# Attention of a fused kernel: sixteen ScalarE exponentials with the row minimum as bias in place of four GpSimd subtractions and four wide exponentials

## The chip, the cores and the metric

The kernel runs on one core of a Trainium2 chip. The metric is the device time of one execution in microseconds, as the median of several runs. The times quoted from the profile come from one profiled execution.

## The reference

The whole computation is a chain of four residual layers on an image `x` of 128 x 128 positions and 64 channels: `x = x + layer(group_norm(x))`. The change lies in the first, an attention along each row of the image with 4 heads of 32:

```python
x = _layernorm(pair, gamma, beta)
q = (x @ Wq).reshape(B, L, L, N_HEAD, D_HID) * SCALING
k = (x @ Wk).reshape(B, L, L, N_HEAD, D_HID)
v = (x @ Wv).reshape(B, L, L, N_HEAD, D_HID)
bias = x @ Wb
gate = jax.nn.sigmoid(x @ Wg + bg)
attn = jnp.einsum('bijhd,bikhd->bijkh', q, k)
attn = attn + bias[:, None]
attn = jax.nn.softmax(attn, axis=-2)
out = jnp.einsum('bijkh,bikhd->bijhd', attn, v).reshape(B, L, L, N_HEAD * D_HID)
out = gate * out
return out @ Wo + bo
```

For each of 128 image rows and each head there is a 128 x 128 matrix of scores, and a softmax over its last axis. All of it is fp32.

## The kernel before

The function `layer0_attention` works on groups of `ROWS` = 4 image rows; there are `GROUPS` = 32 of them. Each engine has its own program, and the programs are held together by semaphores alone. The order of instructions on each engine is written out by hand. In its iteration g an engine works on up to three groups: scores and exponentials of group g, the weighing and the sums of group g - 1, and gate and output of group g - 2.

Of one group:

- TensorE makes the scores of 4 rows and 4 heads (L823, `scores`) into `quad`, one bank for each head.
- VectorE takes head by head (L733, `shift_head`). Four instructions of 128x128 compute bias minus score, write it to `prob` and write the minimum of each line to a column of `least`. After four rows the semaphore `shifted` counts up. This is the negated score, so its minimum is the score's maximum, and the exponential takes `scale=-1.0`.
- GpSimd subtracts the minimum from a whole head, four rows in one instruction of 128x512 (L669), in place in `prob`, and counts `lowered`.
- ScalarE takes the exponential of a whole head, 128x512, in place (L697, `exponentials`), and counts `exps_done`.
- TensorE transposes the probabilities row by row (L831, `turn`), four heads to a bank, with two banks for four rows. ScalarE copies each bank to `pT` (L692, `keep_turn`). The turn of rows 2 and 3 waits for the copies of rows 0 and 1. For row 0, `turn` waits for `exps_done` of head after head.
- TensorE weighs the values (L837, `weigh`) and adds up the probabilities (L845, `add_up`). The sums are transposed (L865), VectorE takes their reciprocals (L756), GpSimd widens them to 128x512 in `rwide` (L675), and TensorE transposes them once more (L876).
- VectorE makes the gate's factor and the gated result (L766, L772), TensorE the output projection (L890), VectorE the residual sum (L778), its statistics (L796) and sums by cell (L797). GpSimd copies the two halves of the finished rows to a second image with the halves swapped (L684).
- For the next group TensorE makes q and k (L807, `project_qk`), which ScalarE keeps with a bias column (L701, L703, `keep_qk`). Gate and v (L813, L816, `project_gv`) go into the same two banks as the turns. ScalarE takes tanh of the gate's half (two of 128x256 with a bias column, L722), and VectorE adds the bias to v (L785) after that tanh.

ScalarE's order in an iteration is: four `keep_turn` of group g - 1, the exponentials of head 0 of group g, `keep_qk(g + 1)`, the exponentials of head 1, the two tanh, the exponentials of heads 2 and 3. TensorE's order is: scores of g, transpose of the sums of g - 2, turns of g - 1, transposes of `rwide`, q and k of g + 1, gate and v of g, output projection of g - 2, weighing and sums of g - 1. GpSimd's order before the change is: subtraction of head 0, the widening for g - 2, subtractions of heads 1 to 3, the two swaps of g - 2.

Of the kernel before, what the change touches and what calls it, by code (L numbers as in the profile page):

```python
# [9 lines left out]
ALU = mybir.AluOpType  # L10
ACT = mybir.ActivationFunctionType
# [3 lines left out]
L = 128  # L15
C = 64
HEADS, HD = 4, 32
ROWS = 4
GROUPS = L // ROWS
# [583 lines left out]
def layer0_attention(nc, m):  # L603
# [11 lines left out]
    prob = [m.nat[:, b * WIDE:(b + 1) * WIDE] for b in range(2)]  # L615
# [5 lines left out]
    least = [m.take(HEADS * ROWS) for _ in range(2)]  # L621
    sums = m.take(128)
    rtotal = m.take(ROWS * HEADS)
    rwide = m.take(CH)
    S = lambda name: m.sem(f"l0_{name}")
    bias_kept, bias_made = S("bias_kept"), S("bias_made")
    qk_made, q_ready, k_ready = S("qk_made"), S("q_ready"), S("k_ready")
    gv_made, v_ready, th_ready = S("gv_made"), S("v_ready"), S("th_ready")
    scores_made, shifted, lowered, exps_done = S("scores_made"), S("shifted"), S("lowered"), S("exps_done")
    turned, kept = S("turned"), S("kept")  # L630
    av_made, sums_made, sums_kept, sums_turned = S("av_made"), S("sums_made"), S("sums_kept"), S("sums_turned")
    rtotal_ready, rwide_ready, r_made, factor_ready, gated_ready = S("rtotal_ready"), S("rwide_ready"), S("r_made"), S("factor_ready"), S("gated_ready")
# [5 lines left out]
    def at(r, h, w=L):  # L638
        return slice((r * HEADS + h) * w, (r * HEADS + h + 1) * w)
# [4 lines left out]
    def of_head(t, h):  # L644

        return t.rearrange("p (r h x) -> p h r x", r=ROWS, h=HEADS)[:, h, :, :]
# [8 lines left out]
    def by_half(t):  # L655
        return t.rearrange("p (h x) -> p h x", h=2)

    with nc.Block() as block:

        @block.gpsimd  # L660
        def _(pool):
            step = m.chain(pool, "pool")
            for g in range(STEPS0):
                b = g % 2
                for h in range(HEADS):
                    if g < GROUPS:
                        pool.wait_ge(shifted, HEADS * g + h + 1)
                        scored = of_head(prob[b], h)
                        pool.tensor_tensor(scored, scored, of_head(least[b], h).broadcast_to([128, ROWS, L]),  # L669
                                           ALU.subtract).then_inc(lowered, 1)  # L670
                    if h == 0 and g >= 2:
                        pool.wait_ge(rtotal_ready, g - 1)
                        if g > 2:
                            pool.wait_ge(r_made, g - 2)
                        pool.tensor_copy(rwide.rearrange("p (x d) -> p x d", d=HD),  # L675
                                         rtotal.unsqueeze(2).broadcast_to([128, ROWS * HEADS, HD])).then_inc(rwide_ready, 1)
                if g >= 2:
                    pool.wait_ge(rwide_ready, g - 1)
                    if g < GROUPS:
                        pool.wait_ge(lowered, HEADS * (g + 1))  # L680
                    pool.wait_ge(x1_ready, g - 1)
                    for e in range(2):
                        there, here = slice(e * C, (e + 1) * C), slice((1 - e) * C, (2 - e) * C)
                        step(pool.tensor_copy(m.pairs(HALF * (g - 2), HALF, m.x1s)[there], m.pairs(HALF * (g - 2), HALF)[here]))  # L684

        @block.scalar
        def _(act):
            def keep_turn(g, r):
                act.wait_ge(turned, 4 * g + r + 1)
                if r == 0 and g > 0:  # L690
                    act.wait_ge(sums_made, g)
                act.activation(pT[r], m.bank[r % 2][:, :], ACT.Copy).then_inc(kept, 1)  # L692

            def exponentials(g, b, h):
                act.wait_ge(lowered, HEADS * g + h + 1)
                t = of_head(prob[b], h)
                act.activation(t, t, ACT.Exp, scale=-1.0).then_inc(exps_done, 1)  # L697

            def keep_qk(g):
                act.wait_ge(qk_made, g + 1)  # L700
                act.activation(by_half(qT[g % 2]), m.quad[:, 0:2, 0:256], ACT.Identity,  # L701
                               bias=m.qkg_bias[:, 0:1]).then_inc(q_ready, 1)
                act.activation(by_half(kT[g % 2]), m.quad[:, 0:2, 256:512], ACT.Identity,  # L703
                               bias=m.qkg_bias[:, 1:2]).then_inc(k_ready, 1)

            keep_qk(0)
            for g in range(GROUPS + 1):
                own, past = g < GROUPS, g >= 1
                if past:
                    for r in range(ROWS):  # L710
                        keep_turn(g - 1, r)
                if own:
                    exponentials(g, g % 2, 0)
                if g + 1 < GROUPS:
                    keep_qk(g + 1)
                if own:
                    exponentials(g, g % 2, 1)
                    act.wait_ge(gv_made, g + 1)
                    if g >= 2:
                        act.wait_ge(factor_ready, g - 1)  # L720
                    for half, bank in enumerate((turn_a, turn_b)):
                        last = act.activation(th[g % 2][:, half * 256:(half + 1) * 256], bank[:, 0:256], ACT.Tanh, scale=0.5,  # L722
                                              bias=m.qkg_bias[:, 2:3])
                    last.then_inc(th_ready, 1)
                    exponentials(g, g % 2, 2)
                    exponentials(g, g % 2, 3)
# [1070 lines left out]
def build(nc, args, out):  # L1797
    with ExitStack() as ctx:
        m = Memory(nc, ctx)
        load_and_prepare(nc, m, args)  # L1800
        group_norm(nc, m, 0)
        layer0_norm(nc, m)
        layer0_attention(nc, m)
        layer1(nc, m)
        layer2(nc, m, args)
        layer3(nc, m, args, out)
# [23 lines left out]
```

## Time and profile before

| | |
|---|---|
| median of 3 runs | 1188.38 us (1185.97 to 1188.86) |
| the profiled execution | 1187.14 us |
| its span, first to last instruction | 1185.3 us |
| mean granted TensorE clock | 0.945 |
| busy: TensorE, VectorE, ScalarE, GpSimd | 1092.6, 743.1, 520.7, 341.0 us |
| attention stage | about 104 to 404 us |

The busy shares are averages over four layers with different limits; a change to one layer is read from the stretch of that layer. In the profile PE is TensorE's matmuls, PEld its weight loads (which overlap them), DVE is VectorE, ACT is ScalarE and POOL is GpSimd. Ends of matmuls are modelled, and neighbouring instructions of one engine can overlap, so that two instructions in a row may take less than twice the time of one. What stands in brackets at the end of a row is the idle time of the engine before it, and who ended it.

### The profile page before, as it was taken

The page shows a single profiled execution, that of the slowest core. Times are in us where ns is not written, and L with a number is a line of the kernel's source. Part 1 is how long each engine was busy: PE and PEld are TensorE (multiplying, and loading weights), DVE is VectorE, ACT ScalarE, POOL GpSimd, SP SyncE. Part 2 cuts the span into 40 slices and gives each one's busy share as a digit, 9 for nine tenths or more (in the row PEclk, how much of TensorE's full clock was granted, in tenths as well). Part 3 has the DMA queues.
Part 4 walks back from the last instruction along what each step waited for, and adds up shares of the span by engine and source line. Part 5 has one row for each costly group of instructions (what it writes and reads, how often), then busy time and mean ns, then how long its engine had stood idle before and what let it go on. Part 6 is the DMA issues. An engine that isn't in the chain of part 4 may idle for free. (4 is left out here: it accounts for less than half of the span.)

```text
span 1185.3 us, 25594 instructions
## 1 busy us (share of the span) xinstructions
PE 1092.6 (92%) x9547; PEld 783.1 (66%) x9547; DVE 743.1 (63%) x3576; ACT 520.7 (44%) x1113; POOL 341.0 (29%) x477
## 2 busy tenths in 40 slices
PE   4898999999999699949999999999999999999688
PEld 3457777777777334437767777677677677677486
DVE  3673777778778522245676676766766766766235
ACT  2364767676676300024444445444444444443200
POOL 0151656665665210000221221221212212212211
PEclk8796999999999889958999999999999999999869
DMA  8000000000000000000000000000000000000012
GB/s 165 1 1 1 2 3 2 2 3 2 2 3 2 1 1 1 1 10 1 1 1 1 2 1 2 1 1 1 1 1 2 1 1 1 1 1 1 1 40 108
DMA packets 10463, 11.09 MB, mean 9 GB/s; under 512 B 3812, under 2 KB 8164, under 8 KB 10340
## 3 DMA queue, kind: packets, MB, share of 16 engines
q1 hardware_dynamic: 8964, 8.87, 2.8%
q8 instruction: 76, 1.25, 0.4%
q10 hardware_dynamic: 1376, 0.59, 0.3%
q14 instruction: 47, 0.39, 0.1%
HBM read 5.14 MB, written 4.23 MB: 8 GB/s over the span
## 5 line engine op out<-in xcount | busy, mean ns | idle before, releaser
L1498 PE MATMUL quad<-theta,nat 128*128 128x512 f32 x512 | 240.7, 593 | 0.0
L669 POOL TENSOR_TENSOR nat<-nat,arena 128x512 f32<-128x512 f32 x128 | 132.6, 1047 | 127.2 <-DVE arena L733 127.2
L1297 POOL TENSOR_TENSOR nat<-nat,const 128x512 f32<-128x512 f32 x32 | 40.6, 1270 | 439.8 <-DVE nat L1436 439.8
L1506 PEld LDWEIGHTS quad<-flat 128*128 128x128 f32 x768 | 104.6, 190 | 46.4 <-ACT flat L1328 25.0
L1498 PEld LDWEIGHTS quad<-theta,nat 128*128 128x128 f32 x512 | 87.5, 191 | 61.7 <-issue 61.7
L1506 PE MATMUL quad<-flat 128*128 128x128 f32 x768 | 123.8, 284 | 2.8 <-ACT flat L1328 1.7
L733 DVE CUSTOM_DVE_ANT_0 nat<-quad,arena 128x128 f32<-128x128 f32 x512 | 113.2, 282 | 7.0 <-PE quad L823 7.0
L1328 ACT ACTIVATE flat<-quad 128x256 f32<-128x256 f32 x192 | 73.3, 382 | 70.6 <-PE quad L1506 56.7
L692 ACT ACTIVATE nat<-bank 128x512 f32<-128x512 f32 x128 | 69.5, 595 | 56.9 <-PE bank L831 56.9
L1405 DVE SCALAR_TENSOR_TENSOR flat<-nat,c,duo 128x128 f32<-128x128 f32 x64 | 22.1, 345 | 101.9 <-PE duo L1515 101.9
L697 ACT ACTIVATE nat<-nat 128x512 f32<-128x512 f32 x128 | 77.3, 634 | 5.6 <-POOL nat L669 5.5
L831 PE MATMUL bank<-const,nat 128*128 128x128 f32 x512 | 69.9, 279 | 8.8 <-ACT nat L692 8.0
L1494 PE MATMUL bank<-nat 128*128 128x128 f32 x512 | 69.2, 279 | 0.3 <-DVE nat L1482 0.3
L831 PEld LDWEIGHTS bank<-const,nat 128*128 128x128 f32 x512 | 55.8, 141 | 18.8 <-ACT nat L692 15.6
L1494 PEld LDWEIGHTS bank<-nat 128*128 128x128 f32 x512 | 63.5, 195 | 0.9 <-DVE nat L1482 0.7
L1386 ACT ACTIVATE nat<-bank 128x512 f32<-128x512 f32 x32 | 19.1, 597 | 87.2 <-PE bank L1603 87.2
L1421 DVE MAX8 arena<-nat 128x8 f32<-128x128 f32 x128 | 27.9, 281 | 44.5 <-ACT nat L1365 44.5
L1453 DVE CUSTOM_DVE_ANT_0 nat<-nat,duo 128x128 f32<-128x128 f32 x128 | 29.2, 283 | 37.4 <-PE duo L1614 37.4
L733 DVE DVE_READ_ACCUMULATOR2_ANT arena<- 128x1 f32 x512 | 42.3, 83 | 0.0
L1310 POOL COPY img<-flat 64x256 f32<-64x256 f32 x64 | 39.6, 619 | 3.9
L807 PE MATMUL quad<-flat,w 64*128 64x256 f32 x256 | 38.2, 419 | 2.3 <-DVE arena L733 2.0
L1410 DVE SCALAR_TENSOR_TENSOR flat<-flat 128x128 f32<-128x128 f32 x64 | 38.3, 599 | 2.2
(390 smaller groups left out, 2271.8 us busy)
## 6 DMA issues: line engine op xcount, KB each, us to landing
out<-nat SPq DMA_DIRECT2D x16, 256.0 KB, 2.0
const<-in_constants ACTq DMA_DIRECT2D x1, 400.5 KB, 3.2
arena<-in_L_conv_Ws SPq DMA_DIRECT2D x1, 240.0 KB
flat<-arena SPq DMA_DIRECT2D x3, 32.0 KB, 4.5
nat<-in_x SPq DMA_DIRECT2D x4, 0.2 KB, 12.0
arena<-in_L_conv_Wq ACTq DMA_DIRECT2D x1, 32.0 KB, 6.7
arena<-in_L_conv_Wk ACTq DMA_DIRECT2D x1, 32.0 KB, 6.4
arena<-in_L_conv_Wv ACTq DMA_DIRECT2D x1, 32.0 KB, 6.1
```

What stands on the lines that cost most here:

```text
L669: pool.tensor_tensor(scored, scored, of_head(least[b], h).broadcast_to([128, ROWS, L]), ALU.subtract).then_inc(lowered, 1)
L692: act.activation(pT[r], m.bank[r % 2][:, :], ACT.Copy).then_inc(kept, 1)
L697: act.activation(t, t, ACT.Exp, scale=-1.0).then_inc(exps_done, 1)
L733: last = dve.tensor_tensor_reduce(prob[b][:, at(r, h)], m.quad[:, h, row(r)], m.bias[:, row(h)], -1.0, BIG, ALU.add, ALU.min, least[b][:, ...
L831: last = pe.transpose(m.bank[r % 2][:, row(h)], prob[g % 2][:, at(r, h)], ident)
L1297: pool.tensor_tensor(quarters(rem), quarters(rem), ident.unsqueeze(1).broadcast_to([128, ROWS, 128]), ALU.add).then_inc(diag_added, 1)
L1310: step(pool.tensor_copy(m.cols3[:, :, ROWS * r + e:ROWS * (r + 1):2].rearrange("p j t -> p t j"), source))
L1328: act.activation(kept, m.quad[:, HALF * half:HALF * (half + 1), place * C:(place + 2) * C], ACT.Copy).then_inc(z_ready[half], 1)
L1410: dve.scalar_tensor_tensor(out=x_of(g, half), in0=held[half], scalar=0.0, in1=x_of(g, half), op0=ALU.max, op1=ALU.add).then_inc(x3_ready[h ...
L1494: last = pe.matmul(B[0][:, col(n)], source[:, col(n)], source[:, col(n)], start=True, stop=True)
L1498: return pe.matmul(m.quad[:, n, :], vT[:, col(n)], m.theta[:, part, :], start=(part == 0), stop=False, skip_group_check=True)
L1506: last = pe.matmul(m.quad[:, row, place * C:(place + 2) * C], a8[g % 2][:, col(row)], zs[half][k % 2][:, n, :], start=False, stop=(k == 2) ...
```

## The change

GpSimd's four subtractions of a group are left out, and with them the semaphore `lowered`. ScalarE now waits for VectorE's `shifted` and takes, for each head, four exponentials of 128x128, one for each row, each with that row's column of `least` as the bias: exp(-t + minimum). `exps_done` counts up after the fourth. GpSimd's widening of the reciprocals and its two swap copies stay, in the same order.

```diff
-                for h in range(HEADS):
-                    if g < GROUPS:
-                        pool.wait_ge(shifted, HEADS * g + h + 1)
-                        scored = of_head(prob[b], h)
-                        pool.tensor_tensor(scored, scored, of_head(least[b], h).broadcast_to([128, ROWS, L]),
-                                           ALU.subtract).then_inc(lowered, 1)
-                    if h == 0 and g >= 2:
-                        pool.wait_ge(rtotal_ready, g - 1)
-                        if g > 2:
-                            pool.wait_ge(r_made, g - 2)
-                        pool.tensor_copy(rwide.rearrange("p (x d) -> p x d", d=HD),
-                                         rtotal.unsqueeze(2).broadcast_to([128, ROWS * HEADS, HD])).then_inc(rwide_ready, 1)
                 if g >= 2:
+                    pool.wait_ge(rtotal_ready, g - 1)
+                    if g > 2:
+                        pool.wait_ge(r_made, g - 2)
+                    pool.tensor_copy(rwide.rearrange("p (x d) -> p x d", d=HD),
+                                     rtotal.unsqueeze(2).broadcast_to([128, ROWS * HEADS, HD])).then_inc(rwide_ready, 1)
                     pool.wait_ge(rwide_ready, g - 1)
-                    if g < GROUPS:
-                        pool.wait_ge(lowered, HEADS * (g + 1))
                     pool.wait_ge(x1_ready, g - 1)
...
             def exponentials(g, b, h):
-                act.wait_ge(lowered, HEADS * g + h + 1)
-                t = of_head(prob[b], h)
-                act.activation(t, t, ACT.Exp, scale=-1.0).then_inc(exps_done, 1)
+                act.wait_ge(shifted, HEADS * g + h + 1)
+                for r in range(ROWS):
+                    t = prob[b][:, at(r, h)]
+                    last = act.activation(t, t, ACT.Exp, scale=-1.0, bias=least[b][:, at(r, h, 1)])
+                last.then_inc(exps_done, 1)
```

## Rows read from the trace of the kernel before

**Rows 1.** Stretch: PE, PEld, DVE, ACT, POOL busy, granted clock, DMA share, GB/s.

```profile
229.86:238.82 8.96, 8.44 (x145) 6.77 (x141) 7.12 (x42) 6.23 (x13) 5.45 (x8) 1.00 0.01 2
```

**Rows 2.** Waits of TensorE, 120 to 388 us: total, times, longest.

```profile
PE duo L876 <- POOL arena L675: 8.1, 30, 0.3
PE bank L831 <- ACT nat L692: 7.5, 30, 0.3
```

**Rows 3.** Groups of instructions, 120 to 388 us: busy, mean ns, idle before.

```profile
L697 ACT ACTIVATE nat<-nat 128x512 f32<-128x512 f32 x121 | 73.0, 634 | 0.1
L692 ACT ACTIVATE nat<-bank 128x512 f32<-128x512 f32 x120 | 65.1, 595 | 54.7 <-PE bank L831 54.7
...
L669 POOL TENSOR_TENSOR nat<-nat,arena 128x512 f32<-128x512 f32 x120 | 124.5, 1047 | 100.2 <-DVE arena L733 100.2
```

**Rows 4.** ScalarE in order of time, one repeat: start us, us, instruction.

```profile
231.76 1.09 ACT L692 ACTIVATE nat<-bank 128x512 f32<-128x512 f32 x2 [1.58 <-PE bank L831]
233.11 1.09 ACT L692 ACTIVATE nat<-bank 128x512 f32<-128x512 f32 x2 [0.26 <-PE bank L831]
234.09 0.62 ACT L697 ACTIVATE nat<-nat 128x512 f32<-128x512 f32 x1
235.60 0.69 ACT L701 ACTIVATE arena<-quad,qkg_bias 128x512 f32<-128x512 f32 x1 [0.89 <-PE quad L807]
...
236.75 0.63 ACT L697 ACTIVATE nat<-nat 128x512 f32<-128x512 f32 x1
237.27 0.84 ACT L722 ACTIVATE arena<-bank,qkg_bias 128x256 f32<-128x256 f32 x2
237.98 1.17 ACT L697 ACTIVATE nat<-nat 128x512 f32<-128x512 f32 x2
```

**Rows 5.** TensorE in order of time, the same repeat.

```profile
231.13 1.04 PE L831 MATMUL bank<-const,nat 128*128 128x128 f32 x8
232.41 1.15 PE L831 MATMUL bank<-const,nat 128*128 128x128 f32 x8 [0.25 <-ACT nat L692]
233.83 0.66 PE L876 MATMUL duo<-const,arena 128*128 128x128 f32 x4 [0.27 <-POOL arena L675]
234.42 1.13 PE L807 MATMUL quad<-flat,w 64*128 64x256 f32 x8
...
238.82 1.17 PE L823 MATMUL quad<-arena 32*128 32x128 f32 x32
```

**Rows 6.** GpSimd in order of time, the same repeat.

```profile
232.18 1.05 POOL L669 TENSOR_TENSOR nat<-nat,arena 128x512 f32<-128x512 f32 x1 [2.26 <-DVE arena L733]
233.17 0.61 POOL L675 COPY arena<-arena 128x512 f32<-128x512 f32 x1
```

**Rows 7.** ScalarE's shorter copies in other stages: one group, two in order of time.

```profile
L1328 ACT ACTIVATE flat<-quad 128x256 f32<-128x256 f32 x192 | 73.3, 382 | 70.6 <-PE quad L1506 56.7 <-PE quad L1498 12.5
...
413.32 0.51 ACT L1106 ACTIVATE nat<-arena 64x128 f32<-64x128 f32 x2
413.54 0.29 ACT L1106 ACTIVATE nat<-arena 64x128 f32<-64x128 f32 x1
```

**Rows 8.** VectorE in order of time, from v to the end of an iteration.

```profile
238.14 0.76 DVE L785 TENSOR_TENSOR arena<-bank,v_bias 128x256 f32<-128x256 f32 x2 [0.60 <-ACT arena L722]
...
239.50 0.40 DVE L797 TENSOR_REDUCE flat<-img 128x4 f32<-128x256 f32 x1
```

**Rows 9.** ScalarE at both ends of the stage: groups 0, 1, 30, 31.

```profile
113.87 0.63 ACT L697 ACTIVATE nat<-nat 128x512 f32<-128x512 f32 x1
...
116.76 1.09 ACT L692 ACTIVATE nat<-bank 128x512 f32<-128x512 f32 x2 [0.50 <-PE bank L831]
...
124.22 1.09 ACT L692 ACTIVATE nat<-bank 128x512 f32<-128x512 f32 x2 [1.00 <-PE bank L831]
...
384.20 1.09 ACT L692 ACTIVATE nat<-bank 128x512 f32<-128x512 f32 x2 [1.58 <-PE bank L831]
...
392.18 1.08 ACT L692 ACTIVATE nat<-bank 128x512 f32<-128x512 f32 x2 [1.18 <-PE bank L831]
```

More of the change, by code:

```diff
@@ L628, in layer0_attention @@
     gv_made, v_ready, th_ready = S("gv_made"), S("v_ready"), S("th_ready")
-    scores_made, shifted, lowered, exps_done = S("scores_made"), S("shifted"), S("lowered"), S("exps_done")
+    scores_made, shifted, exps_done = S("scores_made"), S("shifted"), S("exps_done")
     turned, kept = S("turned"), S("kept")
```

## The prediction

> **What bounds the kernel now.** I read the stretches of the attention stage first, then the groups and the waits inside it, then one group of four rows in order of time. In the steady part the stage repeats itself every 8.96 us. TensorE is busy for 8.44 us of each repeat at a granted clock of 1.00, VectorE for 7.12, ScalarE for 6.23, GpSimd for 5.45 [rows 1]. TensorE's missing 0.52 us are two waits, 30 times each: 0.25 us for ScalarE's copies of the turned probabilities (L692), and 0.27 us for GpSimd's widening of the reciprocals (L675) [rows 2]. So TensorE sets the repeat. ScalarE idles 2.73 us of it, 1.84 of them ahead of L692 and 0.89 ahead of L701 [rows 3, 4].
>
> I measure a repeat from the start of the first L692, called zero (231.76) [rows 4]. ScalarE then runs four copies, with one short wait, until the first exponential at 2.33. It waits for the next group's q and k until 3.84, keeps them until 4.99, takes the second exponential (0.52), the two tanh (0.71) and the last two exponentials, and is through at 7.39 (1.17 after 6.22). The next zero is at 8.965: slack is 1.58. TensorE's transposes begin 0.63 before zero [rows 4, 5].
>
> **What is removed.** GpSimd loses 4 subtractions a group, 1047 ns each [rows 3], 4.2 us a group and 134 us over 32 groups. None of them is the last wait of ScalarE in the steady part: L697's idle there is 0.1 us over 121 instructions [rows 3]. What they do hold is L675. The widening starts at 233.17, right behind the subtraction that began at 232.18, and TensorE's transposes of it start at 233.83 instead of at the end of the turns before them (232.41 + 1.15 = 233.56) [rows 5, 6]. Without the subtraction the widening is ready about 1 us sooner, so this 0.27 us wait goes. With ScalarE out of the way the repeat would be 8.965 - 0.27 = 8.69 us. As TensorE starts a matmul some 0.07 us before the modelled end of the one before it, its later work moves up by up to 0.34.
>
> **What is added.** ScalarE does 16 exponentials of 128x128 a group instead of 4 of 128x512; the elements are the same, the fixed cost is paid 12 times more and each instruction reads its bias from a column of SBUF. No row before has this form. What counts is the distance between the starts of two neighbours, called e here.
> - Elements: copies from PSUM take 595 ns at 512 columns and 382 at 256 [rows 3, 7], 0.832 ns a column, 0.107 us for 128.
> - From the exponentials of now: neighbours start 0.52 to 0.53 us apart (1.17 - 0.634 for the pair, and 0.52 from 236.75 to 237.27). Taking off 384 columns, 0.32, leaves 0.205. The bias: two L701/L703 copies with a bias column take 1.15, 0.575 each, against 0.49 for L692 without one (1.09 - 0.60), so 0.085 more. Together e = 0.29 [rows 3, 4].
> - From the tanh, which have a bias column: 0.71 for two of 256 columns, 0.355 each, less 0.107 is 0.248; they read PSUM, and SBUF against PSUM is 0.035 more (0.525 against 0.49): 0.283 [rows 4].
> - Bounds: 0.248, the tanh without the SBUF term, from below. From above 0.22, the distance of two short copies from SBUF without a bias on 64 partitions [rows 7], plus 0.09 for the bias: 0.31.
> I take 0.29, to which two of the three ways lead. One such instruction alone lasts about 0.634 - 0.32 + 0.09 = 0.40, so the last of a head ends 0.11 after the next could have started.
>
> ScalarE's work grows by 16 x 0.29 - 4 x 0.525 = 2.54 us a group. It had 2.73 us idle, but the idle time doesn't lie where the work goes: the engine takes its instructions in order, and its loop closes over TensorE. Turn of row 0 needs the last exponential of head 3; the first L692 needs that turn; everything else on ScalarE is queued behind it.
>
> **The new repeat, along ScalarE.** From zero: first head of exponentials at 2.33. They no longer wait for GpSimd, and VectorE has had head 0 done long before. They end their slots at 2.33 + 4e = 3.49. q and k of the next group come from TensorE 0.34 sooner, at 3.84 - 0.34 = 3.50, so they no longer hold ScalarE noticeably. Then 1.15 for L701 and L703, 4e, 0.71 for the tanh, 8e, 0.11 for the tail. From the end of an exponential to the first L692: TensorE starts within 0.06 of a ScalarE end (the first L692, of 0.60, ends at 232.36, and the turn that waits for its bank starts at 232.41). The fourth transpose of row 0 starts about 0.33 behind the first (an estimate: eight take 1.04 with the length of the last), at 231.46, and L692 follows at 231.76, 0.30 later [rows 3 to 5]: together 0.36. The sum is 3.50 + 1.15 + 0.71 + 0.11 + 0.36 + 12e = 5.83 + 12e = 9.31. Where q and k are there already it is 2.33 + 1.15 + 0.71 + 0.47 + 16e = 4.66 + 16e = 9.30. Either way ScalarE's loop is longer than TensorE's 8.69, and by it the new repeat is 0.345 us longer than 8.965.
>
> What waits behind: VectorE's L785 needs the tanh, which now end at 3.50 + 1.15 + 1.16 + 0.83 = 6.64. From L785's start to L797's end are 1.76 [rows 8], so VectorE turns to the next scores at 8.4; they are done 8.23 - 0.34 = 7.89 after zero (238.82 + 1.17 in before's times) [rows 5]. Its first two heads then are through some 2 us later, at 1.2 of the next repeat, while ScalarE wants the second at 4.65. VectorE has over 2 us free in 9.31, so it isn't on the path. GpSimd keeps the widening and the two swaps, no bound. TensorE waits once a repeat, for the last exponentials, some 0.6 us, with the work of scores and sums behind it and nothing else delayed.
>
> **The ends of the stage** [rows 9]. First group: the second head of exponentials starts at 113.87 whatever happens before it, as it is behind q and k. Then 12e + 0.71 + 0.47 = 4.66, so the first L692 is at 118.53 instead of 116.76: +1.77. The next interval was 7.46 with no older group's work in it and becomes 4.66 + 16e = 9.30: +1.84. The 29 intervals from 124.22 to 384.20 average 8.965 and become 9.31: +10.0. The last has no q and k to keep: 2.33 + 0.71 + 0.47 + 16e = 8.15 against 392.18 - 384.20 = 7.98: +0.17. Behind it nothing changes. The sum is +13.8 us. The profiled execution took 1187.14 us (span 1185.3), so it would take 1200.9. The median of the runs is 1188.38, 1.24 more; the forecast is 1188.38 + 13.8 = 1202 us.
>
> The time hangs on e with 12 + 16 + 29 x 12 + 16 = 392 of them: 0.01 us is 3.9 us. At e = 0.255 the change is worth nothing.
>
> The Trainium skill, "ScalarE: Activation LUTs", section "What ACT_TABLE_LOAD costs", gives an instruction with a bias column 280 ns and 0.833 ns a column, with neighbours overlapping by about 93 ns. By that estimate e would be 0.294 and the sum +15.4 instead of +13.8. The trace before agrees at 256 columns (0.477 alone would be 0.493 by the page), and has no 128x128 exponential.
>
> **The rivals.**
> 1. Forecast, e from 0.27 to 0.30: 1194 to 1206 us, chance 0.70. Three derivations fall in it.
> 2. Short instructions have a longer floor, as the copies of 128 columns at 0.22 without any bias hint [rows 7]. At e = 0.31 the second form governs, 4.66 + 16 x 0.31 = 9.62: +7.8 for the 392 and +2.0 for 29 intervals at 0.07 more, 1212 us. Against it: those copies have a strided output and 64 partitions. Chance 0.13.
> 3. The bias costs what it costs in the tanh, and SBUF nothing: e = 0.248 to 0.264, 1185.6 to 1192. The removed GpSimd wait and the longer queue cancel. Chance 0.10, most of it within 0.3%.
> 4. The other side: the fetch of the bias is hidden wholly behind the neighbour, e about 0.22 as in those copies. Below 0.255 the change wins, and below 0.239 TensorE's 8.69 bounds again: 29 x -0.275 = -8.0, the start +0.9 and +0.7, 1182 us. For it speaks that a freed wait of 0.27 stands plainly in the trace; against it that L701 and L692, of equal shape, differ by 0.085 between starts, not only in length. Chance 0.07.
> A fall of TensorE's clock through the longer wait gets no chance of its own: its busy share would go from 8.44 of 8.96 us, at a clock of 1.00 [rows 1], to 8.44 of 9.31.
>
> **Chances and range.** Three in a thousand, 3.6 us, is about what a measurement of this kernel can tell from no change. Rivals 1 and 2 are slower by more, 0.83; rival 3 gives 0.08 to the same and 0.01 to either side; rival 4 is faster. So faster 0.08, same 0.08, slower 0.84. The range runs from e = 0.264 (1192) to just below the upper bound's 1212: 1191 to 1211. It leaves out rival 4, most of 3, and the tip of 2.
>
> **What would show it.** Right: first L692 of neighbouring groups 9.2 to 9.4 us apart; exponentials of 128x128 0.28 to 0.30 between starts and about 0.40 long; ScalarE nearly without idle time (some 0.5 us a repeat) and all of it ahead of the first L692; a new wait of TensorE's L831 for ScalarE's exponentials, 0.5 to 0.7 us a group; its wait for L675 gone; VectorE's L733 unchanged. Wrong: neighbours closer than 0.255, then TensorE's wait for the exponentials is small or absent; or VectorE later than I have it, its heads then ending the waits of the exponentials.

## The result and the profile after

The changed kernel takes 1205.08 us (median of 4 runs, 1203.96 to 1206.08), the kernel before 1188.11 us (4 runs). The ratio is 1.0146, with a 95% interval from 1.0128 to 1.0163: 17 us slower. The forecast was 1202, the range 1191 to 1211. The profiled execution after took 1205.16 us, its span is 1203.4.

One repeat of the attention stage after the change, as a stretch (busy PE, PEld, DVE, ACT, POOL, then the granted clock), beside [rows 1]:

```profile
270.03:279.41 9.38, 8.45 (x143) 6.77 (x142) 6.95 (x44) 8.71 (x25) 1.41 (x3) 1.00 0.01 3
```

The repeat went from 8.965 to 9.38 us. TensorE does the same work in it, 8.45 us against 8.44. ScalarE went from 6.23 to 8.71 us, and GpSimd from 5.45 to 1.41. Four microseconds a repeat were taken from an engine whose busy time bounded nothing; only the place of the widening in its order held TensorE up.

The groups of instructions and the waits of TensorE in the steady part, 120 to 398 us, beside [rows 2, 3] (L689 is the new exponential, L683 the copy that was L692, L824 the turn that was L831):

```profile
L689 ACT ACTIVATE nat<-nat,arena 128x128 f32<-128x128 f32 x472 | 147.1, 397 | 0.0
L683 ACT ACTIVATE nat<-bank 128x512 f32<-128x512 f32 x119 | 64.8, 596 | 20.4 <-PE bank L824 20.4
...
PE bank L824 <- ACT nat L689: 20.0, 29, 0.7
...
PE bank L824 <- ACT nat L683: 7.3, 29, 0.3
```

Each exponential lasts 397 ns. ScalarE's only idle time is ahead of L683, and TensorE has a new wait for L689, 0.69 us in each of 29 groups. The wait for the widened reciprocals is gone from the list.

ScalarE in order of time, from one zero to the next, beside [rows 4]:

```profile
270.03 1.09 ACT L683 ACTIVATE nat<-bank 128x512 f32<-128x512 f32 x2 [0.42 <-PE bank L824]
271.37 1.09 ACT L683 ACTIVATE nat<-bank 128x512 f32<-128x512 f32 x2 [0.26 <-PE bank L824]
272.36 1.26 ACT L689 ACTIVATE nat<-nat,arena 128x128 f32<-128x128 f32 x4
273.52 0.67 ACT L694 ACTIVATE arena<-quad,qkg_bias 128x512 f32<-128x512 f32 x1
274.10 0.68 ACT L696 ACTIVATE arena<-quad,qkg_bias 128x512 f32<-128x512 f32 x1
274.67 1.27 ACT L689 ACTIVATE nat<-nat,arena 128x128 f32<-128x128 f32 x4
275.83 0.82 ACT L715 ACTIVATE arena<-bank,qkg_bias 128x256 f32<-128x256 f32 x2
276.55 2.44 ACT L689 ACTIVATE nat<-nat,arena 128x128 f32<-128x128 f32 x8
279.41 1.09 ACT L683 ACTIVATE nat<-bank 128x512 f32<-128x512 f32 x2 [0.42 <-PE bank L824]
```

This is the loop of the prediction. Head 0 starts at 2.33 and takes 1.16, q and k follow without a wait, and the last exponential ends at 8.96. The next zero comes 0.42 later. Neighbouring exponentials start (2.44 - 0.397) / 7 = 0.292 us apart.

TensorE at the end of that loop, beside [rows 5]:

```profile
277.87 0.49 PE L824 MATMUL bank<-const,nat 128*128 128x128 f32 x3
279.04 0.77 PE L824 MATMUL bank<-const,nat 128*128 128x128 f32 x5 [0.69 <-ACT nat L689]
280.06 1.15 PE L824 MATMUL bank<-const,nat 128*128 128x128 f32 x8 [0.25 <-ACT nat L683]
281.04 0.60 PE L869 MATMUL duo<-const,arena 128*128 128x128 f32 x4
```

Three transposes of row 0 run as soon as the sums are turned, and the fourth, that of head 3, waits 0.69 us. This row shows what bounds: of the exponentials, TensorE waits only for the last of sixteen.

### The profile page after: what moved, and what is told of

Read it like the earlier page. It is cut to its first block and busy times, and to the rows that moved or that the text cites. A ratio compares the mean times of both kernels' runs of the same rounds, so it can differ in the third digit from the quotient of the medians.

```text
span 1203.4 us, 25821 instructions
## 1 busy us (share of the span) xinstructions
PE 1096.7 (91%) x9547; PEld 785.2 (65%) x9547; DVE 737.9 (61%) x3576; ACT 600.0 (50%) x1497; POOL 211.8 (18%) x349
## 5 line engine op out<-in xcount | busy, mean ns | idle before, releaser
L689 ACT ACTIVATE nat<-nat,arena 128x128 f32<-128x128 f32 x512 | 159.4, 397 | 3.4 <-DVE arena L726 3.4
L824 PE MATMUL bank<-const,nat 128*128 128x128 f32 x512 | 78.3, 287 | 30.9 <-ACT nat L689 22.0
L824 PEld LDWEIGHTS bank<-const,nat 128*128 128x128 f32 x512 | 55.9, 142 | 48.7 <-ACT nat L689 29.7
L683 ACT ACTIVATE nat<-bank 128x512 f32<-128x512 f32 x128 | 69.8, 596 | 22.4 <-PE bank L824 22.4
L778 DVE TENSOR_TENSOR arena<-bank,v_bias 128x256 f32<-128x256 f32 x64 | 24.2, 419 | 50.3 <-ACT arena L715 50.3
L675 POOL COPY img<-img 64x256 f32<-64x256 f32 x64 | 25.5, 398 | 155.3 <-DVE img L771 153.3
L669 POOL COPY arena<-arena 128x512 f32<-128x512 f32 x32 | 19.5, 610 | 134.8 <-issue 93.8
L1387 ACT ACTIVATE arena<-arena 128x4 f32<-128x4 f32 x32 | 6.6, 205 | 68.2 <-DVE arena L1450 68.2
## 6 DMA issues: line engine op xcount, KB each, us to landing
nat<-in_x SPq DMA_DIRECT2D x4, 0.2 KB, 12.1
```

The lines of the kernel that those rows point to most:

```text
L689: last = act.activation(t, t, ACT.Exp, scale=-1.0, bias=least[b][:, at(r, h, 1)])
L824: last = pe.transpose(m.bank[r % 2][:, row(h)], prob[g % 2][:, at(r, h)], ident)
```

## The experiments

Each run is compared with the kernel before on the same chip. The median of before was 1188.09 us beside the removal, the splitting, the order on GpSimd and the first version with k on VectorE, and 1187.1 us beside two and three split heads, the second version with k on VectorE and the wide first group. "Zero" is, as in the prediction, the start of a group's first copy of turned probabilities on ScalarE.

### The removal alone

This kernel leaves out the subtraction of the minimum altogether.

```diff
 # on the changed kernel
-                for r in range(ROWS):
-                    t = prob[b][:, at(r, h)]
-                    last = act.activation(t, t, ACT.Exp, scale=-1.0, bias=least[b][:, at(r, h, 1)])
-                last.then_inc(exps_done, 1)
+                t = of_head(prob[b], h)
+                act.activation(t, t, ACT.Exp, scale=-1.0).then_inc(exps_done, 1)
```

> The changed kernel with four wide exponentials of 128x512 a group again, without a bias: the subtraction of the minimum is left out of the computation altogether. This is the removal alone. My theory (TensorE bounds once ScalarE is out of the way, and only the wait for the widening went): a repeat of 8.69 us instead of 8.965, some 30 times, 1188 - 8 = 1180 us, TensorE without a wait for L675's successor, VectorE's instructions as long as before. Rival (GpSimd's subtractions slow VectorE or others through shared memory access): VectorE's L733 successor shorter than 281 ns, and more than 10 us gained. Second rival (the widening's wait hides another one right behind it): 1188, no gain.

Measured: 1172.29 us, ratio 0.9861 (0.9842 to 0.988). That is 16 us less, twice what was expected, so the expected size was wrong. The first rival asks for shorter VectorE instructions, and there are none: L724, the renamed L733, takes 282 ns on average in the steady part, as L733 does before. The gain is in the distance between TensorE's starts, which the run "Only the order on GpSimd" shows below.

### The splitting alone

```diff
 # on the kernel before
-                t = of_head(prob[b], h)
-                act.activation(t, t, ACT.Exp, scale=-1.0).then_inc(exps_done, 1)
+                for r in range(ROWS):
+                    t = prob[b][:, at(r, h)]
+                    last = act.activation(t, t, ACT.Exp, scale=-1.0)
+                last.then_inc(exps_done, 1)
```

> The kernel before, with GpSimd's subtractions, but each wide exponential split into four of 128x128 without a bias column. This is the splitting alone. My theory: neighbours start about 0.205 us apart (0.292 measured with the bias, less 0.085); ScalarE's loop is 2.33 + 1.15 + 0.72 + 0.11 + 0.42 + 16 x 0.205 = 8.0 us, under 8.965, so the time stays within 0.3% of 1188. Rival (the number of instructions is the cost, bias or not): starts 0.27 or more apart, the loop 9.1 or more, 1192 us or more.

Measured: 1187.73 us, ratio 0.9996 (0.9985 to 1.0007), no change. Two rows of ScalarE in order of time:

```profile
237.61 0.90 ACT L698 ACTIVATE nat<-nat 128x128 f32<-128x128 f32 x4
...
239.12 1.71 ACT L698 ACTIVATE nat<-nat 128x128 f32<-128x128 f32 x8
```

Four more exponentials take 1.71 - 0.90 = 0.81 us, 0.2025 each. So the splitting costs ScalarE 16 x 0.2025 - 4 x 0.525 = 1.14 us a group. Its idle time takes this in: ahead of the first copy it fell from 1.58 to 0.75 us, ahead of the copy of q from 0.89 to 0.62, and the time didn't move. The bias column accounts for 0.292 - 0.2025 = 0.09 us of an exponential, 1.43 us a group. Laid end to end without any wait for q and k, ScalarE's loop over TensorE is 2.33 + 1.15 + 0.71 + 0.11 + 0.42 + 4 x 0.525 = 6.82 us with wide exponentials. With the splitting it is 7.96, still under the repeat of 8.965; with the bias as well it is 9.39, over it. No run has the bias without the splitting.

### Only the order on GpSimd

```diff
 # on the kernel before, in GpSimd's program
+                if g >= 2:
+                    pool.wait_ge(rtotal_ready, g - 1)
+                    ... the widening, as in the changed kernel
                 for h in range(HEADS):
                     if g < GROUPS:
                         ... the subtraction
-                    if h == 0 and g >= 2:
-                        ... the widening
```

> The kernel before with one move on GpSimd: the widening of the reciprocals stands ahead of the subtraction of head 0 instead of behind it. Four wide exponentials and four subtractions as before. My theory: the 0.27 us wait of TensorE goes, the subtraction of head 0 starts about 0.6 us later and is still through before ScalarE is free for it at 2.33 after zero; a repeat of 8.69, 1180 us. Rival (the later subtractions now hold ScalarE's heads 0 to 2, or the gain of the change's removal needs GpSimd to be empty): a new idle time ahead of ScalarE's exponentials and 1185 us or more.

Measured: 1173.19 us, ratio 0.9874 (0.9854 to 0.9894). That is 15 us less with all four subtractions in place, as much within the noise as the 16 us without any. Here too the expected size, 8 us, was half of what came. Its zeros, and TensorE between them:

```profile
233.82 1.09 ACT L692 ACTIVATE nat<-bank 128x512 f32<-128x512 f32 x2 [1.58 <-PE bank L831]
...
242.30 1.09 ACT L692 ACTIVATE nat<-bank 128x512 f32<-128x512 f32 x2 [1.58 <-PE bank L831]
```

```profile
234.48 1.14 PE L831 MATMUL bank<-const,nat 128*128 128x128 f32 x8 [0.25 <-ACT nat L692]
235.46 0.60 PE L876 MATMUL duo<-const,arena 128*128 128x128 f32 x4
235.99 1.13 PE L807 MATMUL quad<-flat,w 64*128 64x256 f32 x8
```

The repeat is 8.48 us, not 8.69. From the second turn to the transposes of the widened reciprocals there are now 0.98 us between starts against 233.83 - 232.41 = 1.42 before, and from there to q and k 0.53 against 0.59 [rows 5]: 0.50 us in all for a wait that the list of waits gave 0.27. The idle column counts from the modelled end of the turn. Now the transposes start 0.16 us ahead of that end (234.48 + 1.14 = 235.62). Before, they started 0.27 behind it, and they took 0.66 us instead of 0.60. So here the matmul that waits also loses the overlap with its predecessor. With 0.49 instead of 0.27 a repeat, 30 times, the sum is 14.7 us, what the two runs show.

### How many heads can be split

On the kernel with only the order on GpSimd changed, the first n heads are done as in the changed kernel and the others as before. GpSimd subtracts for the heads from n on only; that part is not shown.

```diff
+                t = of_head(prob[b], h)
+                if h < n:
+                    act.wait_ge(shifted, HEADS * g + h + 1)
+                    for r in range(ROWS):
+                        t = prob[b][:, at(r, h)]
+                        last = act.activation(t, t, ACT.Exp, scale=-1.0, bias=least[b][:, at(r, h, 1)])
+                    last.then_inc(exps_done, 1)
+                else:
+                    act.wait_ge(lowered, (HEADS - n) * g + h - n + 1)
+                    act.activation(t, t, ACT.Exp, scale=-1.0).then_inc(exps_done, 1)
```

> Between the two kernels, with the widening first on GpSimd: heads 0 and 1 take four exponentials with the minimum as bias each, heads 2 and 3 keep GpSimd's subtraction and the wide exponential. My theory (ScalarE's loop is 6.82 us for no such head, and 0.64 us more for each, against 8.475 us of TensorE as measured in widening_first): 8.10 us, still hidden, so 1173 us as widening_first. Rival (the cost of the splitting is in proportion to the number of split heads, wherever the bound lies): half of the way from 1173 to 1205, 1189 us.

> As two_heads_bias with head 2 split too, head 3 alone with the subtraction. My theory: ScalarE's loop is 6.82 + 3 x 0.64 = 8.74 us and sets the repeat, 0.27 above TensorE's 8.475: about 1181 us, TensorE's first wait for an exponential back with some 0.3 us. Rival in proportion: 1197 us. Second rival (still hidden): 1173 us.

Measured: two heads 1174.99 us, ratio 0.9894 (0.9876 to 0.9912); three heads 1183.37 us, ratio 0.996 (0.9945 to 0.9974). Zeros of the kernel with two split heads, then of that with three:

```profile
228.28 1.09 ACT L692 ACTIVATE nat<-bank 128x512 f32<-128x512 f32 x2 [0.82 <-PE bank L838]
...
236.75 1.08 ACT L692 ACTIVATE nat<-bank 128x512 f32<-128x512 f32 x2 [0.81 <-PE bank L838]
```

```profile
231.72 1.08 ACT L692 ACTIVATE nat<-bank 128x512 f32<-128x512 f32 x2 [0.42 <-PE bank L838]
...
240.46 1.08 ACT L692 ACTIVATE nat<-bank 128x512 f32<-128x512 f32 x2 [0.42 <-PE bank L838]
```

The repeats are 8.47 and 8.74 us: TensorE's own with two, and 6.82 + 3 x 0.64 = 8.74 of ScalarE's loop with three. With two the first copy still finds ScalarE idle for 0.8 us, so the loop has slack. With three the idle time is down to 0.42, which is the turn-round over TensorE, the same as with four. The wait of TensorE that was expected there shows at its weight loads (8.3 us in 30 groups), not ahead of a matmul. The heads are not in proportion: the first two cost some 2 us of the total, if anything, the third 8, the fourth 22. Most of the last is 0.64 us in each of 29 intervals, and the start of the stage, below, has a share in it.

### Taking load off ScalarE in the changed kernel

```diff
 # on the changed kernel, ScalarE: its copy of k is left for group 0 alone
+                if g == 0:
+                    ... the copy of k
 # VectorE, ahead of head 3
+                if g + 1 < GROUPS:
+                    dve.wait_ge(q_ready, g + 2)
+                    dve.tensor_scalar(by_half(kT[(g + 1) % 2]), m.quad[:, 0:2, 256:512], m.qkg_bias[:, 1:2], None,
+                                      ALU.add).then_inc(k_ready, 1)
```

> The changed kernel with its sixteen exponentials, but the copy of k with its bias (0.57 us between starts) moved from ScalarE to VectorE, ahead of VectorE's head 3, for all groups but the first. My theory (ScalarE's loop of 9.38 us sets the repeat): 9.38 - 0.57 = 8.81 us, 31 times, so 1205 - 17 = 1188 us, with TensorE's wait for the exponentials down from 0.69 us to about 0.1. Rival (VectorE, later than before, is what really delays the exponentials): it gets 0.7 us more work, so no gain or a loss, 1205 us or more, and ScalarE idle ahead of its exponentials.

Measured: 1196.35 us, ratio 1.0064 (1.0047 to 1.0081). Half of the expected gain is missing: the expectation of 1188 us was wrong. VectorE in order of time, and then TensorE:

```profile
234.54 0.75 DVE L769 TENSOR_SCALAR arena<-quad,qkg_bias 128x512 f32<-128x512 f32 x1 [0.52 <-ACT arena L694]
...
236.05 0.48 DVE L776 SCALAR_TENSOR_TENSOR img<-duo,bo,img 128x256 f32<-128x256 f32 x1
```

```profile
236.59 1.08 PE L843 MATMUL duo<-nat,pick 128*32 128x128 f32 x32 [0.48 <-DVE img L776]
```

Here VectorE first waits 0.52 us for ScalarE to have read q, then copies k, then does head 3 and only then the residual sum, which TensorE's sums of the next group wait for, 0.48 us in 27 groups. The repeat is 9.165. The second version puts the residual sum ahead of the copy of k and leaves all else alone:

> k_on_vector with VectorE's order mended: the residual sum first, then the copy of k, then head 3. In k_on_vector the residual sum came late, and TensorE waited 0.48 us a repeat for it (repeat 9.165). My theory (ScalarE's loop bounds once that wait is gone): 9.38 - 0.57 = 8.81 us, 31 times, about 1188 us. Rival (VectorE simply has too much work for a shorter repeat): another of its results is waited for and the repeat stays above 9.0, 1194 us or more.

Measured: 1187.83 us, ratio 0.9998 (0.9988 to 1.0008). Its zeros, and a wait of TensorE between 125 and 380 us:

```profile
232.46 1.08 ACT L683 ACTIVATE nat<-bank 128x512 f32<-128x512 f32 x2 [0.45 <-PE bank L829]
...
241.29 1.08 ACT L683 ACTIVATE nat<-bank 128x512 f32<-128x512 f32 x2 [0.46 <-PE bank L829]
...
PE quad L821 <- DVE arena L727: 8.2, 28, 0.3
```

8.83 us here, for 8.81 expected. ScalarE's loop set the repeat of the changed kernel: taking 0.57 us out of it brought 17 us of time. That the repeat stopped so near 8.81 is in part chance, though. TensorE's wait for the exponentials is gone from the steady part, and instead its scores (L821) wait 0.29 us in each of 28 groups for VectorE's head 3, now behind the copy of k. So a loop over VectorE of 8.83 us bounds here, just over ScalarE's 8.81, and by these rows a larger cut on ScalarE alone would have brought little more.

### The start of the stage

In the profile after, the zeros of groups 0 and 1 lie 10.20 us apart, where the steady repeat is 9.38. In the stretches around them the seventh column is the granted clock:

```profile
116.00:118.00 2.00, 0.70 (x3) 0.34 (x3) 1.75 (x13) 2.00 (x8) 0.00 (x0) 1.00 0.00 0
118.00:120.00 2.00, 1.40 (x6) 1.17 (x7) 2.00 (x21) 1.18 (x4) 0.00 (x0) 0.59 0.00 0
120.00:122.00 2.00, 2.00 (x10) 1.53 (x11) 0.38 (x4) 1.39 (x3) 0.00 (x0) 0.56 0.00 0
```

TensorE is busy for 0.70 of 2 us, and behind that its clock is for the most part at the lower level (0.50 of full speed, 1.2 GHz) for some 4 us; from 122 us on it is 1.00 again. The experiment does group 0 alone in the old way (subtractions on GpSimd, wide exponentials); nothing else differs from the changed kernel.

> The changed kernel, but group 0 alone is done as before: four subtractions on GpSimd and four wide exponentials. In the changed kernel the first interval between the zeros of groups 0 and 1 is 10.20 us against 9.38 later, with TensorE's granted clock at 0.56 to 0.59 from 118 to 122 us. My theory (the long wait of TensorE in the first group takes the clock down, and that costs the 0.8 us): the first zero comes 1.8 us sooner, TensorE's wait of 0.84 us there goes, the clock stays at 1.00 and the next interval is 9.4; together 2.6 us less than the changed kernel, 1202.5 us. Rival (the fall of the clock has nothing to do with that wait): the interval stays at 10.2 and the gain is 1.8 us.

Measured: 1201.13 us, ratio 1.011 (1.0093 to 1.0128), 4 us under the changed kernel. The zeros of groups 0 and 1:

```profile
118.07 1.09 ACT L688 ACTIVATE nat<-bank 128x512 f32<-128x512 f32 x2 [0.50 <-PE bank L834]
...
127.45 1.09 ACT L688 ACTIVATE nat<-bank 128x512 f32<-128x512 f32 x2 [0.42 <-PE bank L834]
```

9.38 us apart, and the clock is at 1.00 in each stretch from 116 us on. That fits the theory; the 4 us of the medians, between forecasts of 2.6 and 1.8, don't decide by themselves. But the first version with k on VectorE had the fall as well (waits of 0.82 and 0.84 us in TensorE's first group), while the second, with waits of 0.95 and 0.84 us, had a clock of 1.00 from 114 us on. Two further kernels waited longer at one time and didn't fall either: two split heads 1.27 us, three split heads 1.45 us. The stretch of the first of them is nearly as idle as that of the changed kernel:

```profile
116.00:118.00 2.00, 0.73 (x10) 0.62 (x7) 1.43 (x9) 1.57 (x4) 0.00 (x0) 1.00 0.00 0
118.00:120.00 2.00, 1.75 (x15) 1.27 (x15) 2.00 (x21) 1.67 (x4) 0.07 (x1) 1.00 0.00 0
```

So the changed kernel itself was run twice more.

> The changed kernel itself once more, for the start of the stage alone. If TensorE's wait in the first group always takes the clock down behind it, the interval between the zeros of groups 0 and 1 is again 10.2 us, with a clock of some 0.5 to 0.6 for about 3 us. Rival (the wait only makes the fall possible, as k_on_vector and k_on_vector_late hint, of which one fell and the other did not): 9.4 us and a clock of 1.00 in at least one of two more executions.

> As changed_again_1, a further execution with a profile: 10.2 us by the theory that the wait always takes the clock down, 9.4 us possible by its rival.

Measured: 1204.2 and 1204.14 us. First two zeros of the one and of the other, with a stretch of each in which the clock is down:

```profile
117.56 1.09 ACT L683 ACTIVATE nat<-bank 128x512 f32<-128x512 f32 x2 [0.42 <-PE bank L824]
...
127.81 1.08 ACT L683 ACTIVATE nat<-bank 128x512 f32<-128x512 f32 x2 [0.42 <-PE bank L824]
...
118.00:120.00 2.00, 1.79 (x8) 1.57 (x8) 0.97 (x10) 1.24 (x3) 0.00 (x0) 0.50 0.00 0
```

```profile
119.57 1.09 ACT L683 ACTIVATE nat<-bank 128x512 f32<-128x512 f32 x2 [0.42 <-PE bank L824]
...
129.92 1.09 ACT L683 ACTIVATE nat<-bank 128x512 f32<-128x512 f32 x2 [0.42 <-PE bank L824]
...
122.00:124.00 2.00, 2.00 (x10) 1.64 (x12) 0.00 (x0) 1.76 (x5) 0.00 (x0) 0.52 0.00 0
```

10.25 and 10.35 us: in all three executions the clock fell behind the first group and the interval was about 0.9 us over the steady one. TensorE's first wait was 1.12, 0.62 and 0.39 us in them, its second 0.84 each time. So for the changed kernel the fall and its price are shown, and in the one execution with a wide first group it didn't come. That the waits as such cause it is not shown: the first two waits come to 1.23 to 1.96 us in the executions that fell and to 1.52 to 1.79 in the three kernels that did not, and the busy share of the stretch doesn't tell them apart either. What does stays open.

## Why the prediction was right

The direction, the place and the mechanism were right; the sum was 13.8 us where the stage grew by 17.1 (from the first copy of q in the stage, 105.07 before and 105.43 after, to the last zero, 392.18 and 409.62). The rows of after for the terms (those of before are in [rows 9]), then term by term:

```profile
105.43 0.69 ACT L694 ACTIVATE arena<-quad,qkg_bias 128x512 f32<-128x512 f32 x1 [10.53 <-PE quad L800]
...
119.11 0.60 ACT L683 ACTIVATE nat<-bank 128x512 f32<-128x512 f32 x1 [0.56 <-PE bank L824]
...
129.31 1.09 ACT L683 ACTIVATE nat<-bank 128x512 f32<-128x512 f32 x2 [0.42 <-PE bank L824]
...
401.39 1.09 ACT L683 ACTIVATE nat<-bank 128x512 f32<-128x512 f32 x2 [0.42 <-PE bank L824]
...
409.62 1.09 ACT L683 ACTIVATE nat<-bank 128x512 f32<-128x512 f32 x2 [0.42 <-PE bank L824]
```

| term | predicted | measured |
|---|---|---|
| first zero later | +1.77 | (119.11 - 105.43) - (116.76 - 105.07) = +1.99 |
| zeros of groups 0 and 1 | +1.84 | 10.20 - 7.46 = +2.74 |
| 29 intervals | +10.0 | 272.08 - 259.98 = +12.1 |
| last interval | +0.17 | 8.23 - 7.98 = +0.25 |

- **The distance e** was taken as 0.29 and is 0.292. It came out of rows of other forms: the element rate from two copies, the fixed part from the wide exponentials (0.205 without the bias, measured 0.2025), and 0.085 for the bias from L701 against L692, measured 0.09. The Trainium skill, "ScalarE: Activation LUTs", section "What ACT_TABLE_LOAD costs", gives 280 ns with a bias column and 186 ns without one, 0.833 ns a column with either, and 93 ns of overlap between neighbours. An estimate by these figures is 0.294 us with the bias and 0.200 without. The runs agree, with 0.292 and 0.2025. The bound of 0.31 from the short strided copies was too high, that of 0.248 too low.
- **The loop over TensorE** of 4.66 + 16e is the step that made the difference between "ScalarE has 2.73 us idle and gets 2.54 more" and a loss. It was confirmed in both directions, by two and three split heads and by the copy of k taken away. Of its terms one was mis-sized: from the end of the last exponential to the zero I had 0.36, and it is 0.42. The 0.30 in it was read where the transposes flow without a wait; behind a wait they take 0.37 (279.04 to 279.41). With some rounding that is 0.07 us a repeat, 2.1 us in 29, two thirds of the 3.3 us that the sum was short by.
- **The slack of 1.58** in the prediction is misread. Of the 1.58 us ahead of zero 0.42 are the turn-round, which no work can fill, and the 0.89 ahead of the copy of q can be filled in part. The slack of the loop is 8.965 - 6.82 = 2.15 us, and the change took 2.57. This cost the forecast nothing, as its sum goes by the loop.
- **The start** was right in its first part: 1.77 predicted, 1.99 measured, of which 0.14 are the clock, already down at 118.60 (in the two repeats the first zero is 13.54 and 13.53 us behind the first copy of q, here 13.68). In the second the 0.9 us of the clock were missing. I had weighed the clock only by the steady share of busy time, and not where the stage is just getting up to speed.
- **The freed wait of L675** was taken as 0.27 us, up to 0.34 with the overlap; it is worth 0.49. This step failed in size, and it cost the forecast nothing, since ScalarE's loop is longer than TensorE's in either case and q and k were there in time in both. It would have mattered in rival 4, whose floor of 8.69 us is really 8.48: had e been 0.22, the kernel would have gained more than the 6 us I gave it. That the error didn't reach the forecast is owed to where the bound lay, not to the reading.
- **VectorE** was rightly off the path: no wait of ScalarE for it is left in the steady part, and it idles over 2 us a repeat. The two versions with k on VectorE show how near it is all the same.
- **ScalarE's idle time** was to be some 0.5 us a repeat, all of it ahead of the first copy. It is 0.68: 0.42 there and 0.26 ahead of the third.

Outside the stage the spans differ by another 1.0 us: 0.36 lie ahead of it, and 0.48 between the last zero and L431 (14.63 against 14.15). The first is less than executions of one kernel differ by: in the two repeats the first copy of q starts at 104.02 and 106.04. The second is in the last output projection, before and after:

```profile
402.57 0.65 PE L890 MATMUL duo<-arena,wo 128*64 128x256 f32 x4 [1.50 <-DVE arena L772]
...
420.01 1.12 PE L883 MATMUL duo<-arena,wo 128*64 128x256 f32 x4 [1.50 <-DVE arena L765]
```

The granted clock was 1.00 in the first and 0.50 in the second. I have no experiment on this.

The best version that computes the whole softmax is the one with only the order on GpSimd changed: 1173.19 us, 1.3% under the kernel before, with one instruction moved. It keeps GpSimd's subtractions, which cost nothing that could be measured (1173.19 us against 1172.29 without them), and takes the one thing that the change had to give.

## What to carry to other kernels

An engine's idle time can't be spent like money: ask where in the loop the work lands, follow the chain from its last instruction over the other engines back to its own first, and compare that loop with the one that sets the repeat. When work is taken from an engine that only held something up through its order, try the order first. Read the worth of a freed TensorE wait from start to start, not from the idle column, and look at the first group by itself.

## What the runs showed of the hardware that was not expected

- A TensorE wait of 0.27 us by the list of waits was worth 0.49 to 0.50 us of the repeat once removed (1.42 to 0.98 and 0.59 to 0.53 us between starts).
- Of TensorE's clock: behind the first group of the changed kernel, with waits of 0.39 to 1.12 and of 0.84 us, it was for the most part at 0.50 for 3 to 4 us in three executions out of three, and the interval took 10.20 to 10.35 us instead of 9.38. In one execution with the first group done in the old way it stayed at 1.00, and so it did in three other kernels, whose first waits were 0.95, 1.27 and 1.45 us.
- The bias column costs ScalarE 0.09 us of distance between neighbours at 128 columns, not only of length: 0.292 against 0.2025.
